# A gated delta rule on one NeuronCore: chunks of 64 tokens with both batches stacked in the partitions, in place of chunks of 128 tokens of one batch

## The reference, cut to what matters

```python
qkvz = hidden_states @ W_qkvz            # q, k, v, z per key head
y = silu(causal_conv4(concat(q, k, v)))  # 4 taps along the tokens, per channel
beta = sigmoid(b); g = -exp(A_log) * softplus(a + dt_bias)
q = l2norm(q) * DK ** (-0.5); k = l2norm(k)
def step(S, inp):                        # one token, every value head
    S = S * exp(gt)
    kv = einsum('hk,hkv->hv', kt, S)
    delta = (vt - kv) * bt
    S = S + kt[:, :, None] * delta[:, None, :]
    o = einsum('hk,hkv->hv', qt, S)
gated = core * silu(z)
gated = gated * rsqrt(mean(gated * gated) + EPS) * norm_w
out = gated @ W_out
```

## Time and profile before

| | |
|---|---|
| runs of the kernel | 3024.3, 3025.3, 3028.1 us; median 3025.31 |
| profiled execution (its span, first to last instruction) | 3029.8 us |
| TensorE busy | 2869.1 us, 95% |
| VectorE busy | 2236.9 us, 74% |
| ScalarE busy | 1953.1 us, 64% |
| GpSimd busy | 1556.2 us, 51% |
| first and last Us of the delta rule | 400.3 and 2677.8 us |

### The profile page before, as it was taken

How to read it: one execution, slowest core, us unless ns; L and a number is a source line. 1 busy time by engine, 2 the same in 40 slices (tenths; PEclk the granted TensorE clock), 3 DMA queues, 4 the chain that set the end, 5 groups by cost and what they waited for, 6 DMA issues and landing times. The chain is left out here.

```text
span 3029.8 us, 70798 instructions
## 1 busy us (share of the span) xinstructions
PE 2869.1 (95%) x22765; PEld 2139.7 (71%) x22765; DVE 2236.9 (74%) x4805; ACT 1953.1 (64%) x6436; POOL 1556.2 (51%) x3618
## 2 busy tenths in 40 slices
PE   5999499999999999999999999999999999879998
PEld 4556267777777777777777777777777777755555
DVE  3443478888888888888888888788888888636776
ACT  3322467777777777777777777777777777532332
POOL 2000466666666666666666666666666666510000
PEclk9999699999999999999999999999999999979999
DMA  3000222223222322222222223222222232110000
GB/s 87 1 1 0 59 62 55 59 52 62 52 59 52 65 63 62 57 55 60 54 62 49 64 55 70 56 60 52 61 53 60 52 63 64 34 43 1 7 8 14
DMA packets 482423, 147.47 MB, mean 49 GB/s; under 512 B 352592, under 2 KB 481216, under 8 KB 482048
## 3 DMA queue, kind: packets, MB, share of 16 engines
q1 hardware_dynamic: 482048, 142.81, 21.9%
HBM read 97.40 MB, written 45.35 MB: 47 GB/s over the span
## 5 line engine op out<-in xcount | busy, mean ns | idle before, releaser
L944 ACT ACTIVATE raw<-bank 128x512 f32<-128x512 f32 x256 | 152.9, 597 | 376.7 <-PE bank L704 335.1
L499 POOL TENSOR_TENSOR Tb<-Tb,btmp 64x14 f32<-64x14 f32 (+6 forms) x896 | 315.6, 352 | 70.9 <-POOL btmp L495 1.1
L495 POOL TENSOR_TENSOR btmp<-Bk,Tb 64x14 f32<-64x14 f32 (+6 forms) x896 | 269.8, 301 | 65.3
L1215 DVE SCALAR_TENSOR_TENSOR conv<-raw,ckq,conv 128x512 f32<-128x512 f32 x384 | 261.6, 749 | 22.1 <-ACT conv L945 20.2
L1215 DVE SCALAR_TENSOR_TENSOR conv<-raw,cv,conv 128x512 f32<-128x512 f32 x384 | 264.2, 753 | 9.8 <-ACT conv L945 7.8
L704 PE MATMUL bank<-xnT,wkq 128*128 128x512 f32 x512 | 253.8, 620 | 13.6 <-POOL mkX L393 7.2
L484 POOL TENSOR_TENSOR Tb<-Bk,lower 64x256 f32<-64x256 f32 x64 | 58.6, 916 | 402.9 <-issue 397.8
L704 PE MATMUL bank<-xnT,wv 128*128 128x512 f32 x512 | 250.5, 612 | 9.4 <-issue 9.4
L772 PE MATMUL bank<-wout_h,gT 128*128 128x256 f32 x1024 | 245.6, 383 | 0.1
L1184 DVE SCALAR_TENSOR_TENSOR S<-S,gs,bank 128x128 f32<-128x128 f32 x512 | 143.8, 343 | 134.2 <-PE bank L743 134.2
L720 PE MATMUL bank<-wz_h,xnT 128*128 128x256 f32 x1024 | 242.4, 380 | 0.0
(11 more groups left out here) (354 smaller groups left out, 7569.6 us busy)
## 6 DMA issues: line engine op xcount, KB each, us to landing
rowb<-decay_rows SPq DMA_DIRECT2D x128, 256.0 KB, 5.1
blk_n<-N SPq DMA_DIRECT2D x128, 256.0 KB, 3.1
Tp<-blk_t SPq DMA_DIRECT2D x128, 128.0 KB, 2.9
Wp<-blk_w SPq DMA_DIRECT2D x128, 128.0 KB, 3.0
wkq<-in_L_attn_W_qkvz_dram SPq DMA_DIRECT2D x32, 128.0 KB, 2.3
wv<-in_L_attn_W_qkvz_dram SPq DMA_DIRECT2D x16, 256.0 KB, 2.7
Bk<-blk_n SPq DMA_DIRECT2D x64, 64.0 KB, 2.7
blk_t<-Tb SPq DMA_DIRECT2D x64, 64.0 KB, 2.5
```

Source lines behind the costliest of these rows:

```text
L495: pool.tensor_tensor(tmp, Bk[:, j, j + 1:].unsqueeze(2).broadcast_to([64, 15 - j, j]), Tb[:, j, 0:j].unsqueeze(1).broadcast_to([64, 15 - j ...
L499: pool.tensor_tensor(Tb[:, j + 1:, 0:j], Tb[:, j + 1:, 0:j], tmp, ALU.subtract).then_inc(row_rdy, 1)
L944: act.activation(raw[h][:, j, :, 3:], bB[1 - j], ACT.Copy)
L1215: dve.scalar_tensor_tensor(out=conv[h][:, j], in0=raw[h][:, j, :, k:k + 256], scalar=cw[:, j, k:k + 1], in1=conv[h][:, j], op0=ALU.mult, o ...
```

## The change

A step still covers a key head and 128 tokens of both batches, but as two halves h of 64 tokens. Partitions 0 to 63 hold batch 0, 64 to 127 batch 1. The four units are now u = 2h + v. N, attn, Wf, ET, ETm, rowb and le4 become `[P, U, 64]`: a 64x64 matrix for each unit and batch. The step from 64 to 128 in the inverse is dropped (x64, w64, xev64, wev64, L616's products, the add into T). The state passes twice in a step: keys, rhs, solve, uscale, increment, update are called with h = 0 and h = 1, queries and from_state too. N is made by four operations with half as many columns; attn by one operation instead of two. xnT keeps the order of the tokens that xnS had, so xnS and GpSimd's copies between them go. raw has a halo in front of each 64 tokens, which ScalarE fills with a third copy in evac; the taps are called per j. The lags from S_L on grow by one, the drain by one slot, RING from 4 to 8; zz and Wf become two buffers. The decays' rows, N's dump and the loads of T and W go as one copy per batch.

```diff
-    S_P, S_S, S_F, S_L, S_D, S_E = 0, 1, 2, 5, 6, 7
-    RING = 4
+    S_P, S_S, S_F, S_L, S_D, S_E = 0, 1, 2, 6, 7, 8
+    RING = 8
...
-                    sp.dma_start(units(nd, U * (t.c % 2), U), N[t.c % RING][:]).then_inc(n_out, 16)
+                    for b in range(B):
+                        sp.dma_start(matrices(nd, U * (t.c % 2), U, b), N[t.c % RING][half[b]]).then_inc(n_out, 16)
...
                 def out_scale(s):
-                    t = s.back(S_D)
+                    t = s.back(S_E)
...
                 def body(s):
                     step_gates(s)
+                    out_scale(s)
                     derive(s)
                     causal(s)
                     halo(s)
                     base_rest(s)
                     base_first(s)
-                    out_scale(s)
                     norm_scale(s)
...
+                def keys(s, h):
...
+                    wait(pe, S_rdy, t.part(h, 1))
+                    for b in range(B):
+                        i = pe.matmul(bank[6][half[b], 0:256], kq_of(t)[:, 0, quarter(t, h), b, :],
+                                      S[:, 2 * b:2 * b + 2, :].rearrange("p v n -> p (v n)"), start=True, stop=True)
+                    i.then_inc(ks_mm, 1)
...
+                    for h in range(2):
                         for b in range(B):
+                            i = pe.matmul(bank[3][half[b], P * h:P * h + P], y[:, 0, quarter(t, h), b, :], y[:, :, quarter(t, h), b, :],
+                                          start=True, stop=True)
...
+                    for v in range(2):
+                        for b in half:
+                            i = pe.matmul(pU[b, v], Wf[t.c % 2][b, 2 * h + v, :], R[b, 2 * h + v, :], start=True, stop=True)
...
+                def increment(s, h):
...
+                    pe.wait_ge(Us_rdy, t.part(h))
+                    pe.wait_ge(oq_rdy, t.part(h))
+                    for v in range(2):
+                        for b in range(B):
+                            i = pe.matmul(pKU[b][:, v], kd[t.c % RING][half[b], 2 * h + v, :], Us[half[b], 2 * h + v, :],
+                                          start=True, stop=True)
...
+                    for u in range(U):
+                        for b in half:
+                            i = pe.matmul(pAU[b, u], attn[t.c % RING][b, u, :], Us[b, u, :], start=True, stop=True)
...
                 def body(s):
                     front_tp(s)
-                    state_in(s)
-                    x64(s)
+                    keys(s, 0)
+                    queries(s, 0)
+                    causal(s)
                     x16(s)
-                    causal(s)
+                    solve(s, 0)
+                    project(s, 0)
+                    increment(s, 0)
                     w1(s)
-                    w64(s)
-                    project(s, 0)
-                    solve(s)
+                    values(s)
+                    project(s, 1)
+                    keys(s, 1)
+                    queries(s, 1)
                     w2(s)
-                    values(s)
-                    apply(s)
-                    project(s, 1)
-                    w3(s)
+                    solve(s, 1)
                     gated_tp(s)
                     zproj(s)
                     low_rank(s)
+                    increment(s, 1)
+                    attend(s)
+                    w3(s)
                     project_out(s)
...
                 def squares(s):
-                    t = s.back(S_D)
+                    t = s.back(S_E)
...
-                    act.activation(raw[h][:, j, :, 3:], bB[1 - j], ACT.Copy)
-                    act.activation(conv[h][:, j], bB[1 - j], ACT.Copy,
+                    new = bank[1 - j][:].rearrange("p (c b n) -> p c b n", c=4, b=B)
+                    act.activation(raw[h][:, j, :, :, 3:], new, ACT.Copy)
+                    act.activation(raw[h][:, j, 1:4, :, 0:3], new[:, 0:3, :, H - 3:], ACT.Copy)
+                    act.activation(conv[h][:, j].rearrange("p c b n -> p (c b n)"), bank[1 - j][:], ACT.Copy,
...
                 def body(s):
-                    ztanh(s)
+                    squares(s)
                     norms(s)
-                    silu(s)
-                    xev64(s)
-                    from_state(s)
+                    from_state(s, 0)
                     normed(s)
-                    wev64(s)
                     evac(s, 0)
                     vscale(s)
                     kdec(s)
                     evac(s, 1)
+                    from_state(s, 1)
                     gtev(s)
-                    squares(s)
                     clamp(s)
                     expo(s)
+                    ztanh(s)
+                    silu(s)
...
                     for u in range(U):
                         i = dve.scalar_tensor_tensor(out=N[t.c % RING][:, u, :], in0=ET[:, u, :],
-                                                     scalar=ty[t.c][:, CC, u:u + 1], in1=bB[3][:, u // 2, 0:P],
+                                                     scalar=ty[t.c][:, CC, u:u + 1], in1=pGram[:, u // 2, 0, :],
...
                 def body(s):
                     gate(s)
+                    rhs(s, 0)
+                    silu(s)
+                    xev16(s)
+                    uscale(s, 0)
                     accumulate(s)
-                    rhs(s)
-                    xev16(s)
-                    silu(s)
+                    update(s, 0)
                     add_w1(s)
+                    tap(s, 0, (2, 1))
                     strict(s)
-                    uscale(s)
+                    rhs(s, 1)
+                    attention(s)
+                    uscale(s, 1)
                     add_w2(s)
-                    update(s)
+                    tap(s, 0, (0,))
+                    tap(s, 1, (2, 1, 0))
+                    update(s, 1)
+                    add_w3(s)
                     output(s)
-                    attention(s)
-                    add_w3(s)
-                    taps(s)
...
-                for j in range(NQ):
-                    pool.wait_ge(group_out, G_XN + KT * (j + 1))
-                    for k in range(KT):
-                        for c in range(2 * j, 2 * j + 2):
-                            cols = slice(256 * c, 256 * c + 256)
-                            pool.tensor_copy(xnT[:, k, cols].rearrange("p (b h n) -> p h b n", b=B, h=2),
-                                             xnS[:, k, cols].rearrange("p (h b n) -> p h b n", b=B, h=2))
```

More of the change, by code:

```diff
@@ L157, in delta_rule @@
         oq = sb("oq", [P, U, P])
-        zz = sb("zz", [P, B, 256])
+        zz = [sb(f"zz{r}", [P, B, 256]) for r in range(2)]
         gat = sb("gat", [P, U, P])
@@ L222, in pipeline @@
                     body(Slot(i, k))
-            for n in range(STEPS, STEPS + 11):
+            for n in range(STEPS, STEPS + 12):
                 body(Slot(None, n))
@@ L551, in state_in, with queries @@
                         return
-                    wait(pe, S_rdy, t.done(1))
-                    wait(pe, gT_rdy, t.done(2))
-                    ends(pe, s, o_rdy, t, 1)
-                    for j, done in enumerate((ks_mm, qs_mm)):
-                        for b in range(B):
-                            i = pe.matmul(bB[6 + j][:, b], chunk(kq_of(t), t, j, b),
-                                          S[:, 2 * b:2 * b + 2, :].rearrange("p v n -> p (v n)"), start=True, stop=True)
-                        i.then_inc(done, 1)
+                    wait(pe, S_rdy, t.part(h, 1))
+                    for b in range(B):
+                        i = pe.matmul(bank[6][half[b], 0:256], kq_of(t)[:, 0, quarter(t, h), b, :],
+                                      S[:, 2 * b:2 * b + 2, :].rearrange("p v n -> p (v n)"), start=True, stop=True)
+                    i.then_inc(ks_mm, 1)
+                def queries(s, h):
+                    t = s.back(S_D)
+                    if not t.live:
+                        return
+                    wait(pe, S_rdy, t.part(h, 1))
+                    for b in range(B):
+                        i = pe.matmul(bank[7][half[b], 256:512], kq_of(t)[:, 1, quarter(t, h), b, :],
+                                      S[:, 2 * b:2 * b + 2, :].rearrange("p v n -> p (v n)"), start=True, stop=True)
+                    i.then_inc(qs_mm, 1)
                 def x16(s):
@@ L586, in w1 @@
                     wait(pe, xs_rdy, done)
-                    wait(pe, xs64_rdy, before)
+                    wait(pe, w3_rdy, before)
                     for u in range(U):
-                        for h in (slice(0, 64), slice(64, P)):
+                        for h in half:
                             i = pe.matmul(bH[4][h, u], Xs[h, u, :], W[h, u, :], start=True, stop=True)
@@ L654, in front_tp @@
                     wait(pe, kd_rdy, t.done(1))
+                    wait(pe, gT_rdy, t.done(S_E + 1 - S_F))
                     for j in range(2):
-                        for b in range(B):
```

(5 more changed lines are left out.)

424 lines of the change are left out of this document (209 added, 215 removed).

## The result

The changed kernel takes 3517.18 us (median of 4 runs, 3514.29 to 3535.69) against 3026.7 us of the kernel before on the same chip: a ratio of 1.1626, 95% interval 1.1596 to 1.1656. It is 490 us slower. The forecast was 3463 us, 3190 to 3720, slower with 0.86: sign and range held, the middle lay 54 us low. The execution profiled took 3514.29 us, its span 3512.5.

The account below looks back on a forecast made before the run. TensorE's own work bound the kernel before; after, a chain through all engines closing in one slot would: 19.3 us, with contention and solves 20.9, with clock 21.5. Over 120 slots plus drain, 3025 + 438 = 3463 us, range 3190 to 3720.

Parts of the forecast that it names:

- TensorE's own work: TensorE's products per slot: dropped products against extra tile-shape changes, from 17.9 down to 16.6 us.
- The cost of the state products: State products on 128x64 tiles, TensorE: side by side cost as before, 1.82 us; one after the other, +1.8.
- the two bounds given: Increments on 64x128 tiles, TensorE: as before if side by side, +0.9 us if one after the other.
- Steps 1 to 4 of the loop: Chain from halo through ScalarE, project j=1, solve h1, output, squares, out_scale and derive to next halo: 19.3 us.
- The 0.08 for the change of tile shape: TensorE, step 2: delay ahead of the second state product behind project j=1, 0.08 us.
- (a) Contention: GpSimd's out_scale slowed beside VectorE's silu: 1.3 us added, 20.6 us from even slot to odd.
- (b) The odd slots: From odd to even slot, N's way through memory and GpSimd's 16x16 solves lie between: 21.1 us.
- (c) The clock: TensorE idles about 4 us ahead of project j=1 and loses clock: 0.6 us taken, bounds nothing and 1.8.
- The sum: About 120 slots at 21.5 instead of 17.93 us plus one drain slot of 10: 438 us added to 3025.
- Narrow tiles one after the other: Rival: TensorE's narrow tiles don't overlap, loop 22.4 us a slot, 3571 us in all; chance 0.12.
- The chain at its floor: Rival: loop without contention or clock loss, 19.3 to 19.9 us a slot, 3190 to 3260 us; chance 0.18.
- The rival on the faster side: A lag misread, so the loop has two slots and TensorE's 16.6 us sets the step: 2873 us; chance 0.12.

Follow-up runs that it names:

- the fastest order: e10_values_early plus, on VectorE, the making of N ahead of the first state update: 2993.92 us.
- e10_values_early: e8_open_vscale_strict with the transposes of the values moved ahead of the first increment and w1 on TensorE: 3005.06 us.
- the filler: Changed kernel plus twelve unread identity products on TensorE between the transposes of the values and project j=1: 3338.77 us.
- the opened loop: Changed kernel with out_scale behind the halo copy on GpSimd, and norms behind its former place but ahead of squares on ScalarE: 3164.34 us.
- e1_scale_late: Changed kernel with out_scale moved behind the halo copy on GpSimd and normed behind kdec on ScalarE: 3195.66 us.
- e12_after_values_early: Changed kernel with only the transposes of the values moved ahead of the first increment and w1 on TensorE: 3554.33 us.
- e6_open_short: Kernel of the opened loop with rows 1 to 13 of the block solves left out on GpSimd: 3092.62 us.
- e8_open_vscale_strict: Kernel of the opened loop with N made ahead of two taps (VectorE) and vscale ahead of the first evacuation (ScalarE): 3094.07 us.

## Why the prediction was right, and where it was off

- **TensorE's own work shrinks and is not the bound.** Right. Foretold were 16.6 us; with TensorE busy 50.80 of 51.01 us the fastest order ran 17.0. The cost of the state products, taken as side by side, held: four of 256 columns on 128x64 tiles start 0.49 us ahead of the next group (1531.51 to 1532.00), against 0.45. The Trainium skill, page TensorEngine Tiling (Array Packing), section Tiling Modes, has such tiles independent of each other, and the trace agrees. The increments did not keep to their price: eight instructions on 64x128 tiles start 0.65 us ahead of the next group (1535.89 to 1536.54), so 1.3 a slot, where the kernel before took 0.92 (L743, 1518.08 to 1519.00). That is between the two bounds given, 0.9 and 1.8, and most of what 17.0 has over 16.6; why was not pursued.
- **Steps 1 to 4 of the loop.** From the halo's end at 1525.47: project j=1 at 2.50 (foretold 2.5); solve h1 at 7.57 (5.9, of which 1.72 is the projection at the lower clock); from solve to gat 6.99 (7.2); squares 1.40 (1.4); out_scale 2.83 (1.94 and contention); derive 1.99 (2.0); mask and halo 0.88 (0.84). No lag was misread. The small copy cost 0.06 in the queue, under the lower bound given, 0.2. The 0.08 for the change of tile shape, which no row of the kernel before shows, is 0.07 in e10_values_early (the second state product 1.89 us behind project j=1, 1543.31 to 1545.20, against the projection's 1.82).
- **(a) Contention**, 1.3 foretold, 0.9 seen in this slot: L500 took 1.10 us (1541.78 to 1542.88) beside VectorE's silu of 1.21 (1541.61 to 1542.82), and 0.20 in the kernels that run it behind the halo copy, where no silu stood beside it. It ended 0.06 us behind the silu. The Trainium skill, page SBUF — State Buffer, section SBUF: two separate sides, says that such a VectorE operation with two inputs in SBUF and a GpSimd operation exclude each other for the whole instruction; the row agrees, and by that rule a short operation costs the rest of the long one.
- **(b) The odd slots.** The path was sized well, N's end 3.7 us behind the halo (3.8), 5.56 to L515 (6.76), and 5.94 for the rows (5.4), but its place in the sum failed: in most odd slots not the solves set the end (GpSimd still waited for the squares in 25 of 32). With the slower clock the loop's own side ended later and covered them, and shortening the solves gave only 27 us. With the clock kept the two are near equal. The terms written down for it add up to 20.96, not to the 21.1 given, which moves the mean of both slots by less than 0.1.
- **(c) The clock** is the term that was mis-sized: "I take 0.6", between 0 and 1.8. It is 1.3 by the slots of the changed kernel and at most 1.5 by the filler. In the slots shown the slow stretch fell not on the idle time but on project j=1, which is in the loop. Without it the forecast was 20.9 and the run with the clock kept shows 20.4. So the middle of the forecast lay as near as it did because two errors partly cancel: the rest of the loop was taken 0.5 us too long and the clock's cost 0.7 to 0.9 too small.
- **The sum.** 120 x (21.5 - 17.93) + 10 = 438 foretold, 490 measured. The loop phase is 464.8 of it. The 16.9 us ahead of the phase, for which nothing was taken, were not pursued.
- **Rivals.** Narrow tiles one after the other: excluded by the 0.49 us. The chain at its floor, 3190 to 3260: the two extras are real, contention by the row of L500 and the clock by the filler and by the slots sorted above. The rival on the faster side failed for the reason given: out_scale does need the same slot's output.
- **Behind the prediction**, the theory of the opened loop failed twice, with slots that stayed at 18.4 us or more where 17.0 to 18.2 and then 17.2 were foretold, each time since one more wait stood behind the one removed: first N through memory, then the transposes right ahead of their reader.

## What to carry to other kernels

When engines run their bodies in order, look for a chain that returns to its own start within one pass: there the time is the sum of its parts, however idle every engine is, and the cheap cure is the order, not less work. Move what nobody in the chain needs behind the chain's links, and a product away from the reader of its evacuated result. Expect the next chain a few tenths to one microsecond below, and price an exchange only against the chain that binds: the same one gave 201 us here and nothing there, or 89 us here and cost 37 there.

## What the runs showed of the hardware

- TensorE can lose its clock to a short idle time in each slot. In the changed kernel TensorE was busy 86% of the window and waited 2.8 us or more ahead of the projection in every slot; in 50 of 64 slots the four products then took 3.4 to 3.75 us, in 14 they took 1.95 or 1.96.
- The length of the wait just ahead does not tell which of the two it will be: 2.92 us were followed by full clock in the changed kernel, 1.60 us by the lower one in e1_scale_late (three rows below, the first from the changed kernel, the second from e1_scale_late, the third from e12_after_values_early). After waits of 1.3 to 1.5 us all products of e6_open_short and e8_open_vscale_strict in the window took 1.95 or 1.96.

```profile
1420.33 1.96 PE L718 MATMUL bank<-xnT,wv 128*128 128x512 f32 x4 [2.92 <-ACT xn L961]
...
1032.22 3.65 PE L718 MATMUL bank<-xnT,wv 128*128 128x512 f32 x4 [1.60 <-ACT xn L961]
...
1573.33 1.96 PE L718 MATMUL bank<-xnT,wv 128*128 128x512 f32 x4 [3.08 <-ACT xn L961]
```

- Products that do nothing, 12 in each slot, made the kernel 178 us faster (one run).
- Small tiles in float32 overlap: sixteen instructions on 64x64 tiles with 64 columns (L643), four on 128x64 tiles with 256 columns (L585) and eight on 64x128 tiles with 128 columns (L761) took 0.51, 0.49 and 0.65 us to the start of the next group. The last is more than half of the 0.92 that eight on whole tiles took in the kernel before (L743).
